# Probabilities times v in three rounded-float passes, with v and ones side by side in the array, and low features streamed from memory

## The reference, cut to what matters

```python
# layer 0: mark the 10240 largest of n*n weighted attention values of each batch
adj = (emb_s * emb_t) * softmax(x) / sqrt(n); diagonal = -inf
x = x + (1.0 where adj is among its top 10240, else 0.0)
# layer 1: 16 heads of 64, no mask
xn = rms_norm(x, g_norm) * (1 + scale) + shift         # scale, shift from cond @ W_emb + b_emb
q, k, v = split(xn @ W_qkv)                            # 1024 x 1024 by 1024 x 3072
q, k = rms_norm(q, g_q), rms_norm(k, g_k)
attn = softmax(q @ k.T * d ** -0.5)                    # 1024 x 1024 per head
o = concat_heads(attn @ v)
x = x + o + o @ W_out
```

## Time and profile before

| | |
|---|---|
| median of 3 runs | 4089.25 us (4086.39 to 4089.74) |
| profiled execution | 4087.43 us, span 4085.7 us |
| PE busy | 3797.2 us (93%) |
| DVE busy | 2589.9 us (63%) |
| ACT busy | 1545.2 us (38%) |
| POOL busy | 1283.3 us (31%) |
| mean granted clock | 0.959 |

### The profile page before, as it was taken

The page is one execution under the profiler, slowest core; times in us unless marked ns, Lnnn a source line. Parts: engine busy times, 40 slices in busy tenths (PEclk is TensorE's granted clock), DMA queues, the critical chain, the costliest instruction groups (busy, mean ns, idle before and its releaser), DMA issues.

```text
span 4085.7 us, 44416 instructions
## 1 busy us (share of the span) xinstructions
PE 3797.2 (93%) x16035; PEld 2457.0 (60%) x16035; DVE 2589.9 (63%) x4521; ACT 1545.2 (38%) x2727; POOL 1283.3 (31%) x1907
## 2 busy tenths in 40 slices
PE   5885899999988899999989899999989899999999
PEld 2334666666644667766644677777644677666744
DVE  8996777777774777777774677777775322322221
ACT  1005444444423444444422444444432344444430
POOL 1005433333303533333312533333312433333310
PEclk9996899999998899999999799999999799999999
DMA  4002010000134000010024100000124100000023
GB/s 156 0 15 103 16 37 21 21 21 21 34 133 147 16 21 21 27 31 21 21 101 154 55 21 21 21 21 21 37 71 161 31 21 21 21 21 21 21 81 99
DMA packets 179360, 195.25 MB, mean 48 GB/s; under 512 B 7576, under 2 KB 137680, under 8 KB 178128
## 3 DMA queue, kind: packets, MB, share of 16 engines
q1 hardware_dynamic: 179152, 192.55, 14.9%
HBM read 144.29 MB, written 48.23 MB: 47 GB/s over the span
## 4 chain that ended last, share of the span: by engine, by line
PE 73%; DVE 14%; ACT 5%; POOL 4%; issue 3%; DMA 1%; SPq 0%; DVEq 0%; POOLq 0%; ACTq 0%
PE pax L1003 24%; PE ppv L1072 18%; PE pst L1058 10%; PE pst L991 10%; PE pax L1038 7%; DVE mx L823 3%; DVE xr L718 3%; DVE trash L683 3%; PE pax L1021 2%; POOL xn L379 1%; PE pax L1046 1%; PE pax L1096 1%; ACT sA L545 1%; ACT pt L552 1%; DVE otok L838 1%
## 5 line engine op out<-in xcount | busy, mean ns | idle before, releaser
L1003 PE MATMUL pax<-wh,xn 128*128 128x384 f32 x3840 | 1058.1, 347 | 11.8 <-issue 8.8
L1072 PE MATMUL ppv<-pt,v 128*65 128x512 f32 x2048 | 987.8, 594 | 1.0 <-DVE otok L838 1.0
L683 DVE TENSOR_SCALAR_CACHE_REDUCE trash<-keys,state 128x2048 uint8<-128x2048 f32 x384 | 899.8, 2343 | 9.9
L823 DVE TENSOR_REDUCE mx<-pax 128x1 f32<-128x512 f32 x960 | 617.9, 685 | 222.6 <-PE pax L1038 202.2
L1003 PEld LDWEIGHTS pax<-wh,xn 128*128 128x128 f32 x3840 | 704.7, 189 | 22.9 <-issue 19.6
L552 ACT ACTIVATE pt<-pst 128x1024 f32<-128x1024 f32 x512 | 524.5, 1024 | 503.9 <-PE pst L1058 445.7
L1003 PE MATMUL pax<-wl,xn 128*128 128x384 f32 x1920 | 649.3, 338 | 0.0
L809 DVE TENSOR_REDUCE ss<-sq 128x4 f32<-128x256 f32 x256 | 107.2, 419 | 782.2 <-ACT sq L527 782.2
L1038 PE MATMUL pax<-sA 65*128 65x512 f32 x960 | 473.3, 540 | 28.3 <-ACT sA L540 17.5
L1072 PEld LDWEIGHTS ppv<-pt,v 128*65 128x65 f32 x2048 | 278.5, 137 | 297.2 <-issue 221.7
L351 POOL TENSOR_TENSOR wl<-wf,wh 128x1024 fp32r<-128x1024 f32 x99 | 235.9, 2387 | 586.1 <-ACT wh L468 586.1
(11 more groups left out here) (139 smaller groups left out, 4445.0 us busy)
## 6 DMA issues: line engine op xcount, KB each, us to landing
wf<-in_L_cond_W_qkv SPq DMA_DIRECT2D x99, 512.0 KB, 5.4
keys<-in_x SPq DMA_DIRECT2D x32, 512.0 KB, 8.9
xin<-in_x SPq DMA_DIRECT2D x32, 512.0 KB, 4.0
out_x<-xin SPq DMA_DIRECT2D x32, 512.0 KB, 2.6
wo<-in_L_cond_W_out SPq DMA_DIRECT2D x4, 4096.0 KB, 13.6
pt<-out_x SPq DMA_DIRECT2D x64, 256.0 KB, 3.9
out_x<-pt SPq DMA_DIRECT2D x64, 256.0 KB, 2.5
oT_scr<-ostg SPq DMA_DIRECT2D x56, 256.0 KB, 2.0
```

What stands on the lines that cost most here:

```text
L683: e.tensor_scalar(trash[:], kv, thr_f, None, ALU.is_ge, ALU.add, accum_out=cnt[:, c:c + 1]).then_inc(z_cnt, 1)
L823: e.tensor_reduce(mx2[:, j // T, j % T, c:c + 1], max_banks(alone, j)[:, c, :], axis=AX, op=ALU.max).then_inc(m_mx, 1)
L1003: i = e.matmul(qkv_bank(alone, t)[:, 0:6 * DH], xn[:, a, k, t * P:(t + 1) * P], w[:, k, :, :].rearrange("p s c -> p (s c)"), start=(k == 0 ...
L1072: i = e.matmul(ppv[0:DH + 1, c, :], v2[:, par, kt, hh, :], pt[:, kt % 2, c * HALF:(c + 1) * HALF], start=(kt == 0), stop=(kt == T - 1))
```

## The change

It has four parts.

1. Values. exp is taken twice from the scores: into ph, rounded, and into pf, exact. Pool subtracts (low), which gives pl. v is split in the same way into vh and vl. The product is vh by ph, vl by ph and vh by pl, in fp32r: six matmuls of 512 columns per key tile. The stationary operand has 128 columns: v of head 0, ones, v of head 1 lie in memory in that order, and beside(...) takes 128 of these 192 columns, so one half of ppv is the head and the other half its sums, repeated 64 times.
2. The end of a head. Heads come out transposed already. Scalar copies the head's rows to ho and the sums' rows to hs, bank by bank (four copies of 64x512); after both heads Vector takes the reciprocal of all of hs (invert, 128x1024) and Pool multiplies (scale). out_tokens, normalise and out_rows are gone. A head's values wait only until its bank is copied (t_mv).
3. Order. prep_tile(gp+1, 0) runs before the steps, so that step t prepares tile t+1; the steps are counted through both heads, and scores run two tiles ahead; the row maxima are laid out in a new table, slots, from step 9.
4. Memory. Only the high features stay on chip. The low ones are stored to memory once per batch (store_xl) and each tile of 512 KB is read again by every pair (load_xl, two buffers). The split weights are stored in batch 0 (keep_w) and read in batches 1 to 3 (load_w), where no engine splits them any more. In the features' second half Vector copies xtmp to xh.

```diff
 class Sync
+        def load_xl(self, gp, t):
+            e, u = self.e, T * gp + t
+            wait(e, a_qkv, u - 1)
+            e.dma_start(xl[:, u % 2].rearrange(...), xl_scr[t]).then_inc(d_xl[u % 2], 16)
+        def store_xl(self, b, g):
+            for k in range(KT):
+                e.wait_ge(f_lo, m + 1)
+                e.dma_start(xl_parts[:, 4 * g:4 * g + 4, k, :], xlo[:, k % 4, :]...).then_inc(d_xst[k % 4], 16)
         def prep_alone(self, b, kb):
+            for t in range(T):
+                if t % 4 == 0:
+                    for r in range(4):
+                        e.wait_ge(d_xst[r], 32 * (2 * b + t // 4 + 1))
+                self.load_xl(gp, t)
+                if t == 1 and kb is not None:
+                    e.wait_ge(f_xr, T * (b + 1))
+                    self.load_keys(kb)
         def pair(self, b, i, par, search, prep, first):
+            if prep:
+                for t in range(3):
+                    self.load_xl(gp + 1, t)
             if not first:
-                for h in range(2):
-                    e.wait_ge(t_oe, 2 * (gp - 1) + h + 1)
+                e.wait_ge(t_on, gp)
+                e.dma_start(oT_pairs[:, i - 1, :], ostg[:]).then_inc(d_ost, 16)
+                for t in range(3, T):
+                    self.load_xl(gp + 1, t)
 class Pool
+            e.tensor_copy(vh[:, par, t, 0:3:2, :], v).then_inc(a_vh, 1)
+            e.tensor_tensor(vl[:, par, t, 0:3:2, :], v, vh[...], ALU.subtract).then_inc(a_vs, 1)
+        def low(self, gp, hh, kt):
+            e.wait_ge(t_ex, CST + w + 1)
+            e.tensor_tensor(pl[:, kt % 2, :], pf[:, kt % 2, :], ph[:, kt % 2, :].bitcast(F32), ALU.subtract).then_inc(t_lo, 1)
+        def scale(self, gp, stored=None):
+            e.wait_ge(t_rc, gp + 1)
+            e.tensor_tensor(ostg[:], ho[:], hs[:], ALU.mult).then_inc(t_on, 1)
         def pair(self, b, i, par, search, prep, first):
+            for t in range(2):
+                self.low(gp, 0, t)
+            if prep:
+                self.prep_tile(gp + 1, 1 - par, 0)
+            for t in range(2 * T):
+                if t + 2 < 2 * T:
+                    self.low(gp, (t + 2) // T, (t + 2) % T)
+                if prep and t + 1 < T:
+                    self.prep_tile(gp + 1, 1 - par, t + 1)
+                if t == 0 and not first:
+                    self.scale(gp - 1, (PAIRS - 1) * b + i - 1)
 class Scalar
         def exp(self, gp, hh, kt):
-            e.activation(pt[:, kt % 2, :], pst[...], ACT.Exp, scale=DH ** -0.5).then_inc(t_ex, 1)
+            e.activation(ph[:, kt % 2, :], src, ACT.Exp, scale=DH ** -0.5).then_inc(t_eh, 1)
+            e.activation(pf[:, kt % 2, :], src, ACT.Exp, scale=DH ** -0.5).then_inc(t_ex, 1)
         def out_move(self, gp, hh):
-            e.activation(heads_t[:], ppv[0:DH + 1, :, :]..., ACT.Copy).then_inc(t_mv, 1)
+            wait(e, t_on, gp)
+            for c in range(2):
+                e.activation(ho[rows, cols], ppv[rows, c, :], ACT.Copy)
+                e.activation(hs[rows, cols], ppv[other, c, :], ACT.Copy).then_inc(t_mv, 1)
         def pair(self, b, i, par, search, prep, first):
+            for t in range(2 * T):
+                if t == T:
+                    self.out_move(gp, 0)
+                if prep and t == 12:
+                    self.max_row(gp + 1, 1 - par, 0)
+                if t + 2 < 2 * T:
+                    self.exp(gp, (t + 2) // T, (t + 2) % T)
+                if prep and 0 < t < T + 1:
+                    self.stack_tile(gp + 1, 1 - par, t - 1)
+                if prep and t + 1 < T:
+                    self.prep_tile(gp + 1, 1 - par, t + 1, z=before[t + 1])
 class Vector
-        def normalise(self, gp, hh):
+        def invert(self, gp):
+            e.wait_ge(t_mv, 4 * gp + 4)
+            e.reciprocal(hs[:], hs[:]).then_inc(t_rc, 1)
         def pair(self, b, i, par, search, prep, first):
+            if not prep:
+                self.invert(gp - 1)
                 if prep:
                     self.prep_sums(gp + 1, t)
+                    if t == 0 and not first:
+                        self.invert(gp - 1)
                     if t > 0:
                         self.prep_split(gp + 1, t - 1)
                     if before is not None:
                         self.search_update(before)
...
+            else:
+                self.invert(gp)
 class Tensor
         def values(...)
+            e.wait_ge(t_eh, w + 1)
+            for m, v in enumerate((vh, vl)):
+                for c in range(2):
+                    if kt == 0 and m == 0:
+                        wait(e, t_mv, 2 * g - 1 + c)
+                    e.matmul(ppv[:, c, :], beside(v, par, kt, hh), ph[:, kt % 2, c * HALF:(c + 1) * HALF], ...)
+            if between is not None:
+                between()
+            e.wait_ge(t_lo, CST + w + 1)
             for c in range(2):
-                i = e.matmul(ppv[0:DH + 1, c, :], v2[:, par, kt, hh, :], pt[:, kt % 2, c * HALF:(c + 1) * HALF], ...)
+                i = e.matmul(ppv[:, c, :], beside(vh, par, kt, hh), pl[:, kt % 2, c * HALF:(c + 1) * HALF], ...)
         def pair(self, b, i, par, search, prep, first):
+            slots = {8: [None, "turn", None], 9: [None, 0, 1], 10: [2, None, 3], 11: [4, 5, 6], 12: [7, None, "row"],
+                     13: [8, 9, 10], 14: [11, 12, 13], 15: [14, 15, None]} if prep else {}
+            self.scores(gp, par, 0, 0)
+            e.wait_ge(t_ex, CST + 2 * T * gp)
+            self.max_row(gp, 1)
+            if prep:
+                self.prep_tile(gp + 1, 0, z=before[0])
+            e.wait_ge(m_ev, 2 * gp + 2)
+            self.scores(gp, par, 0, 1)
+            for t in range(2 * T):
+                gap = slots.get(t, [None] * 3)
+                self.values(gp, par, t // T, t % T, lambda: fill(gap[0]))
+                if t + 2 < 2 * T:
+                    self.scores(gp, par, (t + 2) // T, (t + 2) % T)
+                if prep and 0 < t < T:
+                    self.transpose_tile(gp + 1, t - 1)
+                if prep and t + 1 < T:
+                    self.prep_tile(gp + 1, t + 1, z=before[t + 1])
+                fill(gap[1])
+                fill(gap[2])
```

419 lines of the change are left out of this document (194 added, 225 removed).

## The result

The changed kernel takes 4812.53 us (median of 4, 4801.43 to 4817.16), the kernel before 4089.49 in the same comparison (4086.39 to 4097.56): a ratio of 1.176, 95% interval 1.173 to 1.179. It is slower, as forecast, but by 723 us where 382 were forecast, and outside the range. The profiled execution has a span of 4812.8 against 4085.7, and a mean granted clock of 0.855 against 0.959.

A forecast was written before the change was run, and what follows sets the result against it. TensorE's own work was taken as the bound, busy 93.16 of 94.55 us a pair. Terms 189 + 39 + 16 + 51 + 22 + 38 + 27 = +382 on 4087 gave 4470 us, range 4310 to 4610.

The forecast's parts named there:

- Values: Values of one step on TensorE: six fp32r matmuls take 1.41 us instead of 1.71, 4.8 less a pair.
- Copies: ScalarE's four copies of 64x512 at a head's end: 0.55 us each, bounds 0.38 and 0.60.
- Low: GpSimd's subtractions of 128x1024 for the exps' low parts: 16 more a pair, 2.39 us each.
- The wait at the change of head: TensorE waits for ScalarE's copies, 4.4 us then 0.9; from last qkv tile to first maxima, +6.0 a pair.
- The late read: Low features 3 are read only after the previous pair's store; in batch 3, without search, about +4.4 us.
- Last pairs, start and features: Last pairs +51 us with search and +22 in batch 3; storing and rereading features, keys and weights +38.
- the reciprocal: VectorE's reciprocal of 128x1024: 8.3 us; a rival said 1.2, giving 4338 in all, chance 0.14.
- the wait for the split: First half of a pair with search: TensorE waits 6.8 us for VectorE's split of tile 0, behind reciprocal and counts.
- the second wait of a pair with search: Late read of low features 3 in the first half: about 1.6 us beside the first wait, together +8.4.
- Maxima: Stretch of 16 tiles' row maxima, VectorE and TensorE: 27.2 us instead of 25.8, +1.4 a pair, bounds 24 and 29.
- Clock: TensorE's clock falls after the 6.8 us wait: 1.5 us for each of 18 pairs, +27, bounds 0 and 5 each.
- the clock falls at the head change as well: Rival: the 4.4 us wait also lowers the clock before the first maxima, +4 for 28 pairs, 4580; chance 0.15.

The follow-up runs named there:

- before_burst: Kernel before, one fill() moved so that in steps 2 to 7 of the second half two maxima stand together behind the scores; 4198 us, ratio 1.026 to 1.030.
- rows_64: Kernel before, with the row maxima multiplying 64 rows of sA instead of 65; 4168 us, ratio 1.018 to 1.021.
- f32_values: Changed kernel with values again two fp32 products per tile, one exp, no GpSimd low, v's low part left out; 4770 us.
- f32_even: f32_early with the row maxima placed evenly, as in even_max; 4275 us, ratio 1.045 to 1.048.
- early_even: early_all with the evenly placed maxima of even_max, three passes kept; 4532 us, ratio 1.107 to 1.110.
- f32_early: f32_values with the three waits taken out by order as in early_all; 4459 us, ratio 1.087 to 1.093.
- fill_wait: Changed kernel with 18 unused matmuls of 512 columns before the first values of head 1 in the 28 preparing pairs; 4763 us.
- copies_early: Changed kernel with ScalarE's out_move of head 0 ahead of the exps of tile 9; 4649 us, ratio 1.119 to 1.138.
- early_all: copies_early plus the reciprocal ahead of the sums of tile 0 and the store of ostg behind the reads of low features; 4651 us.
- even_max: Changed kernel with maxima one behind the vh by ph pass, one behind the last values pass, one behind the scores; 4758 us.
- before_waits: Kernel before, with eight more copies of the first head on ScalarE ahead of the real one in all 32 pairs; 4357 us.
- narrow_max: Changed kernel with VectorE's maxima of the pairs reading 128 of 512 columns; 4534 us, one run.
- before_less: Kernel before, without the low-part pass in scores of head 1, tiles 3 to 7, in preparing pairs; 4091 us, ratio 1.000 to 1.002.

## Why the prediction was wrong

Right: the direction, the places of the waits that it named, and many sizes. Values 1.38 (forecast 1.41). Copies 0.59 (0.55). Low 2.38 (2.39). The wait at the change of head 4.18 and 0.36 (4.4 and 0.9). The late read 3.7 in batch 3 (part of 4.4). Last pairs, start and features 136 (111). Less right: the reciprocal took 6.5 (8.3), and with it the wait for the split 4.4 (6.8), and the second wait of a pair with search, 1.6 for the late read, shows in almost none. So these waits were priced too dear by 4 us in a pair with search. The clock took it back: between the last maximum and the last qkv tile a pair has 9.7 us of slow work on average, up to half of it lost, where the forecast had 1.0. That this part came out near the forecast (+2.7 for +2.3) is luck. TensorE has 4.8 us of values less a pair and the kernel is slower all the same: as forecast, the list decides.

Wrong: the step **Maxima**, +1.4, with bounds of 24 and 29. It measured +10.9, which makes 9.5 x 28 = 266 of the 341 us that the forecast lacks. It failed in three places, of which the last is the largest.
- *The places.* I walked through the table and got 27.2 up to the product behind the last tile; at the full clock it is 29.8 so (28.8 between the first and last tile). Back-to-back tiles cost 2.1 in before_burst. I counted VectorE's work and the work of TensorE, not the 0.95 that VectorE starves behind each burst.
- *The rows.* The 64-row maxima are no part of my list at all. They cost 3.1 (rows_64). With 24.9 + 3.1 + 2.1, less the 0.30 x 6 that values save, the sum is 28.3 for 28.8 measured. The sum takes these as adding up, which holds roughly: with bursts and 64 rows the three passes save 2.0 (f32_values against the change), with even places only 0.2 (f32_even against early_even).
- *The clock.* 28.8 at the full clock became 35.8 on average, 7.0 x 28 = 196 us. I priced the clock by single waits of over 4 us. Here it falls again after it had come back, with waits of 0.61 and 0.55 just before, and in f32_early with none over 0.55 in 20 us.

The term **Clock**, 27 us in all, was the same mistake on the larger scale. From the clocks of the two profiles, TensorE spent 2 x (1 - 0.959) x 4085.7 = 335 us at the lower level before and 2 x (1 - 0.855) x 4812.8 = 1396 after. Each slow microsecond of work costs half of itself, so up to 530 us of the 723. The rival "the clock falls at the head change as well" was true (records of 1.06 behind the wait), but small: fill_wait prices it at 1.8 us a pair, where the rival had 4. It is about the 1.5 by which the change of head (+7.5) passed its forecast (+6.0).

What the experiments show of the cause in the stretch: the clock is lost by several things together. Waits ahead alone never lost it, bursts alone lost it in 7 of 27. Of 27 stretches, those within 1 us of the shortest are

| | waits ahead | waits out |
|---|---|---|
| fp32 values, bursts | 3 (f32_values) | 13 (f32_early) |
| fp32 values, even | not run | 27 (f32_even) |
| three passes, bursts | 1 (after) | 9 (copies_early); none under 32.8 (early_all) |
| three passes, even | 10 (even_max) | 12, none over 30.2 (early_even) |

Waits ahead alone: 27 of 27 held in before_waits. Bursts alone: 20 of 27 held in before_burst. All 27 held as well in narrow_max, which leaves the waits ahead and takes VectorE out of the stretch's way.

Firm are the rows with 27 of 27. The others come from one profiled execution each, and stretches with the same waits come out either way (f32_early above). copies_early and early_all have the same waits in the 10 us ahead of the maxima in the pairs with search, and yet 9 stretches of 28.8 to 29.6 in the one against none in the other. So the table does not rank the causes. It also doesn't isolate the three passes, since with them the wait for a split stays.

Open is where exactly it tips: before_burst holds more often with TensorE busy for 89% of the stretch than f32_early with 28.00 of 30.80, 91%, and in f32_early all six stretches of batch 3 hold but 7 of 21 beside the search. I have no run that tells these apart, and the waits in the traces don't either.

## What to carry to other kernels

- Where TensorE and another engine wait for each other in turn, work taken from TensorE may gain nothing (before_less: 2.35 us a pair out, ratio 1.0007) and can cost the clock. Ask what TensorE does with each microsecond that is freed.
- Lay out a producer and its consumer evenly. Moving one call in an otherwise untouched list cost 2.8%, and its sign is that the consumer's idle time grows in pieces as long as the products between.
- Price every edit in the diff, the smallest ones too: 65 rows to 64 was 81 us.

## What the runs showed of the hardware

- A matmul of 64 rows among matmuls of 65 and 128 costs more than one of 65. In rows_64 a tile of 64 rows and half a values step take 1.66 instead of 1.40: 0.13 for each of the two changes between the kinds there. Over the stretch it is 3.1 for some 32 changes, 0.10 each. The Trainium skill, TensorEngine Tiling (Array Packing), Key Properties, says that changing the tiling mode drains TensorE, and under Available Configurations it lists tiles of 64 rows as a mode of their own. The runs fit this; that the drain is what costs the time is not shown.
- The granted clock goes to 1.2 GHz without a long wait near it: in f32_early after 20 us with no wait over 0.55, in the changed kernel for up to 24 us in one piece, in work that is busy for 91% at full speed. The Trainium skill, TensorE: Matmul & The Clock Gate, A second HAM failure mode: psum-queue depth-cycling, has a case of the same kind, in which frequent short idle times between groups of matmuls make the clock alternate. The traces agree.
- The same work with the same waits ahead can keep the clock or lose it (f32_early: 30.8 and 42.0 us).
- Small instructions of VectorE take longer beside GpSimd's subtractions of 128x1024: 1.50 us for one of 0.43 on average, ending with the subtraction (early_all, 2034.54).
- The reciprocal of 128x1024 takes 6.54 us, where the earlier trace rows gave 0.15 and 0.21 for 1 and 8 elements a row: 6.2 ns for each further one, not the 8 that the two small ones suggest. The agreement that the prediction saw in those 8 does not carry over to the long instruction.
